# Twelve F32R products set singly between the fp16 matmuls of a gate/up group, with the orders of four engines rewritten

## The reference

```python
def xattn(inp_q, inp_k, inp_v, Wt, Wp, Wg, Wz, gamma, beta):      # per batch, C=256 rows, d=512, 8 groups of 32 rows
    t, p, g = Wt @ inp_v, Wp @ inp_q, Wg @ inp_k
    att = sum(p * g over a group) * 0.125
    x = Wz[group] @ (att * t)
    xn = (x - mean(group)) / sqrt(var(group) + 1e-5)
    return xn * gamma + beta + inp_v

def ffn(x, w_gate, w_up, w_down):                                  # 512 -> 1408 -> 512
    q = fp4_quant_dequant                                          # blocks of 16: scale = max|x| / 6, round to the FP4 grid
    h = silu(q(x) @ q(w_gate).T) * (q(x) @ q(w_up).T)
    return q(h) @ q(w_down).T

x = x + xattn(layernorm(x), ctx, ctx, ...)                         # x, ctx: 32 x 256 x 512 float32
x = x + ffn(layernorm(x), ...)
```

## Time and profile before

| what | value |
|---|---|
| median of 3 runs | 1742.09 us (1741.19 to 1744.41) |
| span of the profiled execution, first to last instruction | 1739.4 us |
| TensorE matmul busy | 1682.5 us, 97% of the span |
| VectorE busy | 1518.6 us, 87% |
| ScalarE busy | 825.6 us, 47% |
| GpSimd busy | 707.2 us, 41% |
| chain that ended last | TensorE 94%, VectorE 2%, ScalarE 2% |
| granted TensorE clock, mean | 0.997 |

### The profile page before, as it was taken

How to read it: one execution, slowest core, us unless ns; L and a number is a source line. 1 busy time by engine, 2 the same in 40 slices (tenths; PEclk the granted TensorE clock), 3 DMA queues, 4 the chain that set the end, 5 groups by cost and what they waited for, 6 DMA issues and landing times.

```text
span 1739.4 us, 27808 instructions
## 1 busy us (share of the span) xinstructions
PE 1682.5 (97%) x8723; PEld 922.4 (53%) x8723; DVE 1518.6 (87%) x2577; ACT 825.6 (47%) x1472; POOL 707.2 (41%) x879
## 2 busy tenths in 40 slices
PE   2789999999999999999999999999999999999999
PEld 1666555555555555555555555555555555555544
DVE  8987888889888888988888898888888988888887
...
DMA packets 412150, 155.86 MB, mean 90 GB/s; under 512 B 383200, under 2 KB 384480, under 8 KB 412128
## 3 DMA queue, kind: packets, MB, share of 16 engines
...
## 4 chain that ended last, share of the span: by engine, by line
PE 94%; DVE 2%; ACT 2%; DMA 1%; issue 1%; POOL 0%; SPq 0%; DVEq 0%; ACTq 0%
PE pairs L550 52%; PE work L561 25%; PE work L500 5%; PE work L512 3%; PE ubank L527 2%; PE work L527 2%; PE pairs L605 1%; PE pairs L500 0%; PE pairs L597 0%; DMA hT_parts<-raw 0%; DMA raw<-in_L_ffn_w_gate 0%; DVE w_rinv L1205 0%; DVE x_in L1223 0%; PE pairs L607 0%; PE pairs L580 0%
## 5 line engine op out<-in xcount | busy, mean ns | idle before, releaser
L550 PE MATMUL pairs<-w_gate_hi,xT_parts 128*128 128x512 f16 (+1 forms) x1536 | 555.4, 362 | 1.8 <-DMA xT_parts<-raw 1.5
L550 PE MATMUL pairs<-w_up_hi,xT_parts 128*128 128x512 f16 (+1 forms) x1536 | 554.7, 361 | 0.0
L561 PE MATMUL work<-w_parts,hT_parts 128*128 128x512 f16 x2079 | 458.9, 379 | 0.9 <-DMA hT_parts<-raw 0.9
L561 PEld LDWEIGHTS work<-w_parts,hT_parts 128*128 128x128 f16 x2079 | 203.5, 99 | 236.1 <-issue 1.1
L550 PE MATMUL pairs<-w_up_lo,xT_parts 128*128 128x512 f16 (+1 forms) x768 | 277.5, 361 | 0.0
L550 PE MATMUL pairs<-w_gate_lo,xT_parts 128*128 128x512 f16 (+1 forms) x768 | 277.4, 361 | 0.0
L550 PEld LDWEIGHTS pairs<-w_gate_hi,xT_parts 128*128 128x128 f16 x1536 | 152.7, 99 | 163.2 <-issue 15.1
L550 PEld LDWEIGHTS pairs<-w_up_hi,xT_parts 128*128 128x128 f16 x1536 | 150.3, 98 | 146.5
L964 ACT ACTIVATE early<-pairs,w_unit 128x512 f32<-128x512 f32 (+1 forms) x192 | 124.9, 651 | 166.3 <-PE pairs L550 166.3
L873 ACT CAST raw<-hq 128x704 f16<-128x704 f32 x126 | 98.1, 779 | 179.5 <-DVE hq L1201 178.7
L1409 DVE SCALAR_TENSOR_TENSOR h<-pairs,w_unit,early 128x512 f32<-128x512 f32 (+1 forms) x192 | 135.0, 703 | 39.9 <-ACT early L964 34.6
...
## 6 DMA issues: line engine op xcount, KB each, us to landing
...
```

The lines of the kernel that those rows point to most:

```text
L550: mm = pe.matmul(pairs[:, pair, n, 0:b - a], xT[s][part][:, k, :], w1[n][wpart][:, k, a:b], start=(k == 0 and part == 0 and wpart == 0), s ...
L561: mm = pe.matmul(obank[:, :], hT[part][:, k, :], w2[wpart][:, k, :], start=(k == 0 and part == 0 and wpart == 0), stop=(k == KH - 1 and pa ...
```

## The change

`u_rows` is taken apart into `u_first` and `u_second` (the waits) and `u_part` (one product). A new `hidden_and_u(j, s, c, b)` runs the gate/up group of 24 fp16 matmuls and puts one F32R product behind every second of them, twelve in all. In the body it takes the place of `hidden(j, 0, 0)`, and `mixed` follows it. `output(j-1)` moves behind `hidden(j+1, 1, 0)`. The last body keeps `hidden`. The orders of SyncE, ScalarE, VectorE and GpSimd in the body are written anew; no step is added or taken away. The diff, cut to its core:

```diff
+            def u_first(b):
+                pe.wait_ge(c_ready, HT * b + HT)
+                at_least(pe, u_copied, HT * b)
+                at_least(pe, w_ready, b)
+                at_least(pe, rowst_ready, HT * b)
+            def u_second(b):
+                pe.wait_ge(gram_copied, HT * b + HT)
+            def u_part(b, s, k, wpart, part):
+                mm = pe.matmul(u_bank(b, s), wuT[wpart][:, k, s * P:(s + 1) * P], c_wide[part][:, k, :],
+                               start=(k == 0 and wpart == 0 and part == 0), stop=(k == HT - 1 and wpart == 1))
+                if k == HT - 1 and wpart == 1:
+                    mm.then_inc(u_done, 1)
...
+            def hidden_and_u(j, s, c, b):
+                pair = pair_of(j, s, c)
+                first, last = SPANS[c]
+                u_first(b)
+                for k in range(KD):
+                    if k == KD // 2:
+                        u_second(b)
+                    for part, wpart in PARTS:
+                        for n in range(2):
+                            mm = pe.matmul(pairs[:, pair, n, 0:last - first], xT[s][part][:, k, :],
+                                           w1[n][wpart][:, k, first:last],
+                                           start=(k == 0 and part == 0 and wpart == 0), stop=(k == KD - 1 and part == 1))
+                        if k == KD - 1 and part == 1:
+                            mm.then_inc(gu_done, 1)
+                        u_part(b, k // HT, k % HT, part, wpart)
...
@@ TensorE, body @@
-                pe.wait_ge(x_turned, 16 * (j) + 16)
-                pe.wait_ge(h_done, GROUPS * (j - 1) + 2)
-                hidden(j, 0, 0)
-                if more:
+                    pe.wait_ge(x_turned, 16 * (j) + 16)
+                    pe.wait_ge(h_done, GROUPS * (j - 1) + 2)
+                    hidden_and_u(j, 0, 0, i + 1)
                     mixed(i + 1)
-                    u_rows(i + 1, 0)
-                    u_rows(i + 1, 1)
+                if not more:
+                    hidden(j, 0, 0)
...
-                output(j - 1)
                 pe.wait_ge(x_turned, 16 * (j + 1) + 16)
                 pe.wait_ge(h_done, GROUPS * (j) + 2)
                 hidden(j + 1, 1, 0)
+                output(j - 1)
...
@@ ScalarE, body @@
+                h_hi(j, 0)
+                silu_group(j + 1, 1, 0)
+                h_hi(j, 1)
                 if ahead:
                     ctx_fit_lo(i + 2)
-                grain_h(j)
...
@@ VectorE, body @@
                 h_quant(j, 0)
+                if more:
+                    normalise2(j + 2)
                 h_quant(j, 1)
+                if more:
+                    x_first(j + 2)
                 h_lo(j, 0)
+                gated(j + 1, 1, 0)
+                if more:
+                    x_scales(j + 2)
+                emit(j - 1, 1, 16 * (i - 1))
                 h_lo(j, 1)
...
@@ GpSimd, body @@
                     ctx_root(i + 2)
+                    ln1(i + 2)
                 columns(i + 1)
+                columns_affine(i + 1)
+                if ahead:
+                    add_ctx(i + 2, 0)
+                root2(j + 2)
                 if ahead:
                     ctx_lo(i + 2, 0)
-                columns_affine(i + 1)
-                if ahead:
                     ctx_lo(i + 2, 1)
-                    add_ctx(i + 2, 0)
-                    ln1(i + 2)
-                root2(j + 2)
```

110 lines of the change are left out of this document (49 added, 61 removed).

## The result

The changed kernel takes 1903.95 us in the median of 4 runs (1902.51 to 1904.91), the kernel before 1742.03. The ratio is 1.0929, with a 95% interval from 1.0914 to 1.0945. That is slower, as forecast, and at the upper end of the range of 1775 to 1905: 162 us where the sum said 126. From one `gram` to the next, the first passes left out, a pass of the loop lasts 55.95 us on average (54.90 to 57.65), against 50.33 before (50.31 to 50.39). That is 5.62 us more in each of 29, where the sum said 4.3.

A forecast was written before the change was run, and what follows sets the result against it. TensorE, 97% busy, was taken to bound the loop, with 0.53 us slack for hT_parts. Terms 0.2 - 0.1 + 3.42 + 0.8 = 4.3 us in 29 passes, some 1.1 in the last, gave 126 us more: 1868 us, range 1775 to 1905.

The forecast's parts named there:

- (a): Late hT_parts transpose each pass: 4.3 us more, from 3.3 to 5.5; 1840 to 1905 us; chance 0.56.
- F32R products: TensorE's twelve products between fp16 matmuls: 3.05 us against 2.82 a batch, bounds -0.23 to +0.23, taken as +0.2.
- four steps in the chain: VectorE, before the last h_lo(j): normalise2, x_first, gated(j+1,1,0) and x_scales add 2.31 us.
- two `ctx_lo` collisions: GpSimd's two ctx_lo block VectorE steps around h_quant and normalise2: 2 x 1.17 = 2.34 us.
- slack: Between the landing of hT_parts' transpose at 868.99 and output(j)'s start at 869.52: 0.53 us of lateness absorbed.
- `qT`: Operand due before gram, via turn_q(i+2) behind turn_x(j+2): 13.2 us against 12.4, so 0.8 us more.
- exit row: Profile row of the last F32R product, followed by fp16: 0.254 us a product, applied to all twelve.
- With no slack left: SyncE: turn_c's issue, some 1.9 us, ends just as turn_h(j)'s data is ready; cost put at 0.
- (e): More than 1905 us, if turn_c is late and pushes turn_h, or xT_parts is late for hidden(j+1,1,0); chance 0.05.
- (b): Chain late, but GpSimd slips through or one ctx_lo collides: 1.1 to 3.2 us a pass, 1775 to 1838; chance 0.25.
- third collision: VectorE's steps before turn_q collide with GpSimd's add_ctx: 1.17 us, lengthening 3.56 to 4.73 us.
- the first way: From the last h_lo(j) over output(j) to the next gram: 0.07 + 5.2 + 7.13 = 12.4 us.

The follow-up runs named there:

- run 5: Changed kernel with twelve extra fp16 matmuls filling TensorE's pause ahead of output(j)'s wait for hT_parts; results unread: 1876.7 us.
- run 1: Changed kernel with TensorE's body as before, the other four engines keeping the new orders: 1935.53 us, ratio 1.1098.
- run 3: Changed kernel with VectorE's normalise2, x_first, gated(j+1,1,0) and x_scales moved back behind the last h_lo(j): 1876.4 us, ratio 1.0767.
- run 10: Changed kernel with output(j-1) back ahead of hidden(j+1,1,0): 1938.81 us, ratio 1.1139.
- run 11: Changed kernel with twelve extra matmuls filling TensorE's pause, and turn_c(i+2) moved behind turn_h(j) on SyncE: 1876.19 us, ratio 1.0776.
- run 4: Changed kernel with the context steps of batch i+2 (ctx_fit, ctx_hi, ctx_fit_lo, ctx_lo) early again on ScalarE and GpSimd: 1864.26 us, ratio 1.0702.
- run 8: Kernel before with both ctx_lo behind root2(j+2), ctx_fit_lo behind the SiLU of (j+1,1,0), turn_c behind turn_h(j): 1791.2 us, ratio 1.0289.
- run 6: Changed kernel with the four VectorE steps back behind the last h_lo(j) and the context steps early again: 1864.97 us, ratio 1.0709.
- run 2: Kernel before with F32R products between the fp16 matmuls, mixed behind them, output(j-1) unmoved, two sum_pg behind x_back(j+1): 1753.12 us, ratio 1.0061.
- run 7: Kernel before with the four VectorE steps between h_quant(j,0) and the last h_lo(j), ScalarE's h_hi(j,1) behind gated's SiLU: 1864.76 us, ratio 1.0715.
- run 9: Changed kernel, four steps and context moved back, plus normalise1 before x steps, q_hi before grain_x, turn_q before turn_x: 1759.58 us, ratio 1.0107.

## Why the prediction was right, step by step

The likeliest case, (a), is what happened: a late transpose of `hT_parts` in every pass, with both `ctx_lo` in the chain. Its sum was 36 us too small. The range held with luck: the time lies 1 us below its upper end, and the 5.62 us a pass are above the 5.5 that (a) allowed. That upper end stood for a fourth collision. What used up the room was something else, the granted clock, for which the prediction had no term. With the clock kept up (run 5) the time is 1876.7 us, 9 above the sum. In that remainder too, errors offset each other: `qT` and the collisions came out smaller than forecast, the landing and the short waits had been put at 0. By its terms, for one pass:

| term | forecast | measured | read from |
|---|---|---|---|
| F32R products | +0.2 | +0.11 | 15.03 against 14.92 us |
| wait behind `gram` | -0.1 | -0.11 | step of 0.109 us |
| four steps in the chain | +2.31 | +2.31 | same durations |
| scale step | -0.7 | -0.68 | 870.05 |
| two `ctx_lo` collisions | +2.34 | +2.01 | 879.45, 880.87 |
| `add_ctx` on `h_snap_add`, short waits for ScalarE and GpSimd | 0 | +0.6 | 875.02, the chain's rest |
| issue and landing of `turn_h` | 0 | +0.46 | `turn_c` in flight |
| slack | -0.53 | -0.36 | 0.50 in the mean, 0.14 of it stay |
| `qT` | +0.8 | +0.1 | 0.3 where the clock holds |
| granted clock | not in it | +1.2 | 0.427 us matmuls |
| sum | +4.3 | +5.6 | passes: +5.62 |

- **The F32R products.** The bounds held (-0.23 to +0.23), but the account was wrong in part. A product between fp16 matmuls costs 0.246 us, a little less than the exit row said. The price of before was too low: 11 x 0.233 + 0.254 = 2.82 took the first of the twelve for one like the others, and it takes 0.42 us. They are not dearer now (2.95 against 2.99); the 0.11 come with `mixed`. The rule of the Trainium skill ("TensorE: Matmul & The Clock Gate", section "Wait — 56ns, not 53.3ns?") would have put them at the price of an fp16 matmul; the trace does not agree, with 0.246 against 0.216 us.
- **The chain.** The steps and both collisions are there with the sizes that the rows gave. TensorE's lateness at `output(j)` is 4.34 us, 25.86 us from `group_spread` to `output(j)` against 21.52; 3.42 had been forecast. It is paid in two places, 0.4 at `hidden(j+1,1,2)` and 3.9 at `output(j)`. The slack was counted as 0.53 us, but 0.14 us always lie between a landing and the first matmul that waits for it, and only 0.36 could be used. "With no slack left" for `turn_c` was right for the queue, which costs 0.06 us, and wrong for the landing: I put 0 and it is 0.4 (5.62 against 5.22 us in the mean). Case (e) named `turn_c` as what may push `turn_h`; in the changed kernel it does not, but in runs 1, 3 and 10 it does, by 1.0 to 1.2 us. Run 11 shows the landing doubly: it is real in the landing and worth nothing in time as long as `qT` is due right behind.
- **Who gets in first.** The case (b), in which GpSimd slips through, did not occur. `add_ctx`, of the same kind, also hit `h_snap_add` and `normalise1`. The rule in the Trainium skill ("SBUF — State Buffer", section "Who interferes with whom") says that the later of the two engines is blocked for the whole instruction of the other. The trace agrees: `normalise2` starts 0.45 us behind the first `ctx_lo` and takes 1.49 us in place of 0.54. In run 4 the stall is gone with the `ctx_lo`, and in run 8 it comes with them into the kernel before.
- **`qT`.** The third collision (1.50 us at 888.02) came, with 0.95 of the 1.17 us that were counted. The excess over the first way is 0.3 us and not 0.8, mainly because that way is 0.46 longer by its issue and landing; where run 11 takes 0.28 of this away, `gram` starts 0.62 us late. Run 6 shows how little I had seen of it: with `hT_parts` on time this way alone would have cost 2.5 us a pass.
- **The granted clock.** This is the term that was missing, and the largest part of the error. The prediction took the busy time of TensorE as given and only asked how long it would stand still. Run 5 prices it: 27 us of the 162.
- **What the change gives.** Run 10 shows that the new place of `output(j-1)`, which I put at nothing, saves 35 us among the new orders. It hides a wait that I had not looked for. That it costs nothing by itself is not shown: no run moves it alone in the kernel before.

The sum in the other direction: the four other orders alone cost 194 us (run 1), TensorE's order without the move of `output(j-1)` costs 11 (run 2), and that move gives back 35 (run 10). The parts of the orders do not add up: the four steps alone cost 123 us in the kernel before (run 7), 1.38 us a pass of it for a wait that the change lacks, and give back 28 where they are taken out of the changed one (run 3), because `turn_c`, `gated` and `qT` are late there as well; with the context they give back 39 (run 6); the third layer gives 105 (run 9).
